# The two ends of a causal attention stage: no stacks to fill, matmuls over 48 and 51 rows, the second sequence prepared between the first one's maxima, the last two sequences written out

## The reference, cut to what matters

```python
qkv = jnp.einsum('bsi,oi->bso', layernorm(x), W_qkv)      # B = 16, S = 512, 128 channels
Q, K, V = heads(qkv)                                      # 16 heads of 8 channels
Q, K = apply_rope(Q), apply_rope(K)
scores = jnp.einsum('bhqd,bhkd->bhqk', Q, K) / sqrt(8)
scores = where(causal, scores, -inf)
out = softmax(scores, -1) @ V
x = x + out.reshape(B, S, 128) @ W_o.T
```

## Time and profile before

| | |
|---|---|
| median of three executions | 2770.93 us |
| the profiled execution's own time | 2778.27 us |
| its span | 2776.3 us |
| busy: PE, DVE, ACT, POOL | 82%, 71%, 52%, 45% |
| attention, first DVE instruction | 120.98 us |
| attention, first matmul of the loop | 208.85 us |
| attention, last DVE instruction starts | 1072.74 us |
| next stage, first DVE instruction | 1081.88 us |

### The profile page before, as it was taken

The page is one execution under the profiler, slowest core; times in us unless marked ns, Lnnn a source line. Parts: engine busy times, 40 slices in busy tenths (PEclk is TensorE's granted clock), DMA queues, the critical chain, the costliest instruction groups (busy, mean ns, idle before and its releaser), DMA issues. The chain is left out here.

```text
span 2776.3 us, 50795 instructions
## 1 busy us (share of the span) xinstructions
PE 2284.9 (82%) x14828; PEld 1682.9 (61%) x14828; DVE 1964.2 (71%) x5225; ACT 1446.4 (52%) x2918; POOL 1258.7 (45%) x1094
## 2 busy tenths in 40 slices
PE   6559998999899896768898989488987889898990
PEld 5425555555555554756776777367776667677770
DVE  6766676676676665778786766368887877776775
ACT  4205454454554554756665656355553767565660
POOL 3242322231231222527773555457775387645551
PEclk8759999999999998888899999789999888999995
DMA  2022122122212213411125656310100011356656
GB/s 66 15 36 35 25 36 36 26 31 34 33 25 36 37 25 81 159 54 35 43 73 181 215 205 214 103 31 23 30 15 22 22 39 42 127 187 213 213 198 182
DMA packets 140590, 222.36 MB, mean 80 GB/s; under 512 B 21326, under 2 KB 100992, under 8 KB 129883
## 3 DMA queue, kind: packets, MB, share of 16 engines
q1 hardware_dynamic: 122203, 185.46, 24.7%
q0 software_dynamic: 18176, 34.14, 3.6%
HBM read 136.75 MB, written 57.32 MB: 70 GB/s over the span
## 5 line engine op out<-in xcount | busy, mean ns | idle before, releaser
L955 DVE TENSOR_REDUCE attn_rowmax<-psum 128x1 f32<-128x512 f32 (+3 forms) x748 | 457.5, 637 | 262.0 <-PE psum L796 259.2
L740 ACT ACTIVATE attn_probs<-psum 128x512 f32<-128x512 f32 (+1 forms) x704 | 385.2, 560 | 463.8 <-PE psum L859 453.6
L794 PE MATMUL psum<-attn_ks,attn_qs 72*128 72x512 bf16 (+3 forms) x1088 | 314.0, 324 | 32.5 <-DVE attn_rowmax L955 25.9
L857 PE MATMUL psum<-attn_qs,attn_ks 75*128 75x512 bf16 (+3 forms) x1024 | 290.5, 316 | 32.1 <-issue 19.7
L1290 POOL DMA_INDIRECT experts_answers<-ffn1a_y_rows,ffn1a_out_row x156 | 156.1, 1001 | 150.9 <-ACT ffn1a_y_rows L1360 110.8
L796 PE MATMUL psum<-attn_mask_qk,attn_ident_b 128*128 128x128 bf16 x1088 | 224.0, 231 | 0.0
L1290 POOL DMA_INDIRECT experts_answers<-ffn1b_y_rows,ffn1b_out_row x156 | 154.3, 989 | 147.7 <-ACT ffn1b_y_rows L1360 109.9
L655 POOL TENSOR_TENSOR attn_rstd<-attn_var_eps,minus_half 128x4 f32<-128x4 f32 x18 | 18.3, 1018 | 423.7 <-DVE attn_var_eps L932 423.7
L859 PE MATMUL psum<-attn_mask_kq,attn_ident_b 128*128 128x128 bf16 x1024 | 206.3, 226 | 0.0
L794 PEld LDWEIGHTS psum<-attn_ks,attn_qs 72*128 72x128 bf16 x1088 | 112.6, 103 | 135.2 <-DVE attn_rowmax L955 82.4
L1658 DVE TENSOR_TENSOR ffn1a_hl<-ffn1a_h,ffn1a_hh 128x1024 fp32r<-128x1024 f32 x142 | 174.0, 1225 | 11.3 <-issue 0.9
(11 more groups left out here) (425 smaller groups left out, 6447.7 us busy)
## 6 DMA issues: line engine op xcount, KB each, us to landing
ffn1a_w_ring<-experts_packed SPq DMA_DIRECT2D x39, 1026.5 KB, 5.1
ffn1b_w_ring<-experts_packed SPq DMA_DIRECT2D x39, 1026.5 KB, 5.1
attn_qs<-attn_qparts SPq DMA_DIRECT2D x216, 64.0 KB
attn_ks<-attn_kparts SPq DMA_DIRECT2D x216, 64.0 KB
ffn1a_x_in<-experts_slots SPq DMA_DIRECT2D x39, 264.0 KB, 4.8
ffn1b_x_in<-experts_slots SPq DMA_DIRECT2D x39, 264.0 KB, 4.8
gla_answers<-experts_answers SPq DMA_DIRECT2D x32, 256.0 KB, 3.1
ffn1b_h<-experts_answers SPq DMA_DIRECT2D x16, 512.0 KB, 5.5
```

The lines of the kernel that those rows point to most:

```text
L740: act.activation(probs[:, slot_of(j), 0:n], ps_exp[j % 2][:, 0:n], ACT.Exp, scale=SCALE).then_inc(exp_ready, 1)
L794: pe.matmul(out, qs[k][0:K_QK, 4 * g + hh, qt * P:(qt + 1) * P], ks[k][0:K_QK, 4 * g + hh, 0:n_keys], start=True, stop=False)
L857: pe.matmul(out, ks[k][:, 4 * g + hh, kt * P:(kt + 1) * P], qs[k][:, 4 * g + hh, kt * P:N], start=True, stop=False)
L955: dve.tensor_reduce(rowmax[:, NT - 1 - w, h:h + len(heads)], score_bank(n, j)[:, 0:len(heads) * width_of(w)].rearrange("p (a c) -> p a c", ...
```

## The change

1. `K_QK` becomes 48 and `K_ALL` 51. The maxima's parts stand in rows 48 to 50. No stack is filled any more: a new array `minus_one` (3 x 16 x 512, bf16) is sent to rows 48 to 50 of both `ks` by two more DMAs at the start. `set_values` keeps the memsets of `v_aug`. In the built program each matmul carries the part of the array that it uses: for `score` and `exponent` that was 128 x 128 and is 64 x 128 now; the mask matmuls between them stay at 128 x 128.
2. POOL splits the first sequence's queries and keys in one go. The second sequence's `turn`, `project`, `values`, `normalise_x` and `rotate` move in between the first one's 44 units.
3. The body becomes a function `sequence(i, k, following, prepare)`. The loop has seven bodies, and sequences 14 and 15 are written out: 14 prepares nothing, 15 neither prepares nor scores. `is_first` asks for n == 0, since numbers are now given for the last ones too.

```diff
-    K_QK = 72
+    K_QK = len(PAIRS) * DH
@@ SP
+            for k in range(2):
+                sp.dma_start(ks[k][K_QK:K_ALL, :, :], w["minus_one"]).then_inc(weights_in, 16)
...
-            sp.wait_ge(stacks_set[0], 4)
             stack(0, 0, 1)
             stack(1, 0, 1)
-            sp.wait_ge(stacks_set[1], 4)
             stack(0, 1, 2)
             maxima(0, 0, 0)
             stack(1, 1, 2)
-            with sp.Fori(0, BODIES) as i:
+            with sp.Fori(0, BODIES - 1) as i:
...
+            maxima(1, 0, NB - 2)
+            maxima(0, 1, NB - 1)
+            maxima(1, 1, NB - 1)
             for f in range(2):
-                sp.wait_ge(stack_in[f], 16 * BLOCKS * (NB + 2))
+                sp.wait_ge(stack_in[f], 16 * BLOCKS * NB)
@@ POOL
             inverse_std(1)
-            set_stacks(pool, 0, ((ks, -1.0),), True)
-            split(1, None, (0,))
+            set_values(pool, 0)
+            split(1, None)
             inverse_std(2)
-            split(1, None, (1,))
-            set_stacks(pool, 1, ((ks, -1.0),), True)
+            set_values(pool, 1)
             split(2, 1)
@@ PE, ahead of the loop
-            for k in range(2):
-                turn(k + 1)
...
+            turn(1)
+            pe.wait_ge(weights_in, N_WEIGHTS)
+            project(0, 1)
+            project(1, 1)
+            values(1)
             for j in range(UNITS):
                 score(0, 0, j)
+                if j == E_TURN:
+                    pe.wait_ge(v_read, 1)
+                    turn(2)
+                if j == E_Q:
+                    project(0, 2)
+                if j == E_K:
+                    project(1, 2)
+                if j == E_V:
+                    values(2)
@@ PE, DVE and ACT, in a sequence
                     for j in range(UNITS):
                         exponent(j)
-                        score(1 - k, s + 1, j)
+                    if following:
+                        score(1 - k, s + 1, j)
...
-                        if j == E_TURN:
+                    if j == E_TURN and prepare:
                             turn(s + 3)
...
+            with pe.Fori(0, BODIES - 1) as i:
+                for k in range(2):
+                    sequence(i, k, True, True)
+            sequence(BODIES - 1, 0, True, False)
+            sequence(BODIES - 1, 1, False, False)
```

More of the change, by code:

```diff
@@ L554, in attention_stage @@
         weights_in = sem("weights_in")
-        stacks_set = [sem(f"stacks_set{k}") for k in range(2)]
+        values_set = [sem(f"values_set{k}") for k in range(2)]
         var_ready = sem("var_ready")
@@ L636, in _, with set_values @@
                             maxima(0, 1 - k, i * 2 + (k + 1))
+            maxima(1, 0, NB - 2)
+            maxima(0, 1, NB - 1)
+            maxima(1, 1, NB - 1)
             for f in range(2):
-                sp.wait_ge(stack_in[f], 16 * BLOCKS * (NB + 2))
[L639 to L649, removed]
+                sp.wait_ge(stack_in[f], 16 * BLOCKS * NB)
+                sp.wait_ge(m_in[f], 16 * NB)
+        def set_values(engine, k):
+            engine.memset(v_aug[k][:, :, :, :], 0.0).then_inc(values_set[k], 1)
+            engine.drain()
+            engine.memset(v_aug[k][:, :, :, DH:DH + 1], 1.0).then_inc(values_set[k], 1)
         @block.gpsimd
@@ new lines, in sequence, with read_o @@
+            def sequence(i, k, following, prepare):
+                s = i * 2 + k
+                def read_o(g):
+                    act.wait_ge(pv_done, s * GROUPS + (g + 3))
+                    act.wait_ge(oT_psum, s * 4 + (g + 2))
+                    act.activation(oT[:, :], ps_o[g % 2], ACT.Copy).then_inc(o_read, 1)
+                for j in range(UNITS):
+                    g, (kt, heads) = j // RING, FILLS[j % RING]
+                    n = len(heads) * width_of(kt)
+                    act.wait_ge(exp_psum, s * UNITS + (j + 1))
+                    if j % RING == 0:
+                        act.wait_ge(pv_done, s * GROUPS + (g + 1))
+                    act.activation(probs[:, slot_of(j), 0:n], ps_exp[j % 2][:, 0:n], ACT.Exp,
+                                   scale=SCALE).then_inc(exp_ready, 1)
+                    if j == 0:
+                        end_of(s)
+                    if j == 2 and following:
+                        values(1 - k)
+                    if j == A_TOKENS:
+                        tokens_of(s)
+                    if j == A_TURN and prepare:
+                        turn(s + 3)
+                    if j == A_V and prepare:
+                        read_v(s + 3)
+                    if j in A_O:
+                        read_o(A_O.index(j))
@@ L843, in _ @@
             pe.wait_ge(mT_ready, 1)
-            with pe.Fori(0, BODIES) as i:
-                for k in range(2):
[L846 to L892, removed]
-                        score(1 - k, s + 1, j)
[L894 to L903, removed]
-                        if j == E_TURN:
-                            turn(s + 3)
-                        if j == E_Q:
-                            project(0, s + 3)
-                        if j == E_K:
-                            project(1, s + 3)
-                        if j == E_V:
-                            values(s + 3)
-                        if j == E_HALF:
-                            pe.wait_ge(v_read, s + 3)
-                            turn_maxima(0, s + 1)
-                        if j in E_O:
-                            turn_o(E_O.index(j))
-                    weigh(GROUPS - 1)
@@ L1002, in _ @@
             dve.drain()
-            for s in range(2):
-                moments(s * NT)
-                normalise_x(s * NT, s + 1)
-                if s == 0:
-                    set_stacks(dve, 0, ((qs, 0.0),), False)
-                    dve.wait_ge(weights_in, N_WEIGHTS)
-                rotate(0, s + 1)
-                rotate(1, s + 1)
-            set_stacks(dve, 1, ((qs, 0.0),), False)
+            moments(0)
+            normalise_x(0, 1)
+            dve.wait_ge(weights_in, N_WEIGHTS)
+            rotate(0, 1)
+            rotate(1, 1)
+            moments(NT)
             for j in range(UNITS):
                 row_max(0, j)
+                if j == V_NORM:
+                    normalise_x(NT, 2)
+                if j in (V_Q, V_Q + 1):
+                    rotate(0, 2, (j - V_Q,))
+                if j in (V_K, V_K + 1):
+                    rotate(1, 2, (j - V_K,))
                 if j == UNITS // 2 - 1:
@@ new lines, in sequence @@
+            def sequence(i, k, following, prepare):
+                s = i * 2 + k
+                for j in range(UNITS):
+                    if following:
+                        row_max(s + 1, j)
+                    if j == 1 and prepare:
+                        moments((s + 2) * NT)
+                    if j == V_MAXIMA:
+                        read_maxima(1, s)
+                    if j == V_LAST_O:
+                        normalise(o_heads, channels_of(3), s * 4 + 2)
+                    if j == V_NORM and prepare:
+                        normalise_x((s + 2) * NT, s + 3)
+                    if j == V_OUT:
+                        add_out(s)
+                    if j in (V_Q, V_Q + 1) and prepare:
+                        rotate(0, s + 3, (j - V_Q,))
+                    if j in (V_K, V_K + 1) and prepare:
+                        rotate(1, s + 3, (j - V_K,))
+                    if j in V_O:
+                        g = V_O.index(j)
+                        normalise(o_heads, channels_of(g), s * 4 + (g + 3))
+                    if j == V_HALF and following:
+                        split_maxima(0)
+                    if j == V_HALF_READ and following:
+                        read_maxima(0, s + 1)
+                if following:
+                    split_maxima(1)
@@ L1046, in _ @@
+            with dve.Fori(0, BODIES - 1) as i:
+                for k in range(2):
+                    sequence(i, k, True, True)
+            sequence(BODIES - 1, 0, True, False)
+            sequence(BODIES - 1, 1, False, False)
             normalise(o_heads, channels_of(3), NB * 4 + 2)
@@ L2207, in layout @@
     c["mask_qk"] = np.triu(np.full((P, P), BIG, np.float32), 1).astype(bf)
+    c["minus_one"] = np.full((3, 16, SEQ), -1.0, np.float32).astype(bf)
     c["mask_kq"] = np.tril(np.full((P, P), BIG, np.float32), -1).astype(bf)
```

148 lines of the change are left out of this document (79 added, 69 removed).

## The result

The changed kernel takes 3402.26 us (median of 4, 3391.31 to 3414.93), 1.228 times the kernel before (interval 1.2249 to 1.2314), against a forecast of 3053 us in a range up to 3200. In that comparison the kernel before took 2769.51 us: 633 us more, where I had forecast 282. Direction and place were right, the size was less than half of what came.

What follows compares the result with a forecast made beforehand. PE was taken to bound the loop. Start +9.5, tile changes +293, sequence 14 -4, sequence 15 -11 and handover -5.5 gave +282 on the median 2770.9: 3053 us, range 2738 to 3200 (8 in 10).

Steps and rivals of the forecast that it cites:

- the price of a change: PE's score and exponent matmuls against masks: each change of tile size costs 0.09 us, 256 a sequence, 23.0 us.
- +19.5 for sequences 0 to 14: Loop sequences: 23.0 us of tile changes less 3.5 in PE's waits, +19.5 each, +293 us over 15.
- rival C: A change dearer than between column tiles (3337 us at 0.16), or the clock falls (3250 at three tenths); chance 0.14.
- Part 2, the start: First sequence: first score at 162.3, exponent 2 us earlier, then tile changes of +11.5; together +9.5 us.
- my 39.3: First maxima, with the second sequence's preparation between them: 29.3 us plus 10, from 162.3 to 201.6.
- my 4.5 to 6.6: Start: the DMA of the maxima's parts goes at about 202 and lands 4.5 to 6.6 us later.
- my 11.5: Start: 128 changes of tile size at 0.09 us each, +11.5 us.
- Part 3, the end: Sequence 14 without preparation -4 us, sequence 15 without scores -11 with tile changes, handover to the next stage -5.5.
- -9.5 for -4: Sequence 14: dropping its preparation was to save 4 us, after what lay in waits.
- My 34 for it: Sequence 15 without tile changes: ACT bounds it at 34 us where 53.1 was taken before, so -19.
- Rival B: Changes between row tiles are free, so only the two ends count: -30.5 us, 2740 in all; chance 0.18.
- my 42: Sequence 15 with tile changes: PE bounds it at 42 us, so -11.

Runs made afterwards that it cites:

- ends_75: The changed kernel with 72 and 75 rows again, filled by four DMAs at the start, both ends still changed: 2732.9 us, 0.990 of the kernel before.
- rows_48: The kernel before with only the rows changed, to 48 and 51, old ends kept: 3451.3 us, 1.250 of the kernel before.
- mask_64: The changed kernel with each mask matmul cut into two over 64 rows: 2952.4 us, 1.069 of the kernel before.
- ends_128: The changed kernel with both ends kept and rows filled up to 125 and 128 with zeros against minus ones: 2720.6 us, 2716.1 when run again.
- tail_75: The kernel before with only the last two sequences written out, old start and 72 and 75 rows kept: 2736.1 us, 0.990 of the kernel before.

## Why the prediction was wrong

**Part 1, the direction and the price of a change: right.** I took 0.09 us from column tiles; it is 0.10, by the starts, at the upper clock level and 0.11 at the lower (a pair of L797 and L799 takes 0.76 us from 160.76 to 161.52 in the changed kernel; the same pair takes 0.53 in ends_75: 160.30 to 160.83). The drain that the Trainium skill states in TensorEngine Tiling (Array Packing), Key Properties, holds for rows as well: the trace agrees, with the overlap at 0.07 us in place of 0.16. Nearly all of today's waits were used up: L797's waits for the maxima are gone. The changes are 252 more a sequence, from 8 to 260: so far 252 x 0.105 - 3.5 = 23.0 us a sequence instead of 19.5.

**Part 1, "+19.5 for sequences 0 to 14": the step that failed.** Between ends_75 and the changed kernel the start of sequence 14 moves from 943.3 - 203.8 = 739.5 us to 1540.4 - 214.8 = 1325.6 behind that of sequence 0: 41.9 us a sequence. 23.0 are the changes. The other 18.9, some 280 us over 15 sequences, are what is left, and the clock is the term that the sum put at nothing: 0.653 for 0.961. I had the clock in rival C, with a price of 65 us for each tenth of the time at 0.50, a chance of 0.14 for the whole rival and three tenths as its example, and left it out of the forecast because no row tied it to the change. With its two levels at 1.00 and 0.50, a mean of 0.653 is 0.69 of the time at 0.50, and 0.961 is 0.08: six tenths more, 400 us by that price. So the price was high enough, and the share was what I had not seen coming. rows_48 shows the loss of time and of clock with the rows alone, mask_64 that the clock falls with few changes too, ends_128 that it goes with the rows in use. What it follows in the changed kernel, the gaps at the changes or the smaller part of the array, no run separates. Rows 6 held a warning: PE ran without a gap at 0.50 over 72 rows, so a PE without gaps was not enough to bring the clock up.

**Part 2, the start.** `xn` 2.4 us for 3, the first score at 160.8 for 162.3, the DMA of the maxima at once: right. Without the changes of tile I had -2; it is -4 (ends_75 against tail_75). The maxima with the preparation between them take 39.6 us in ends_75 (159.81 to 199.40) for my 39.3; most of the other two us are in the DMA of the maxima, issued at 199.83 and landed by 202.98, in 3.2 us for my 4.5 to 6.6. That the length came right is partly luck: PE was not fully busy there before, as I had it (5.4 us of the 8 from 182 to 190), and in ends_75 the clock rises for a while (0.91 from 170 to 174), where in tail_75 it stays at 0.50 up to the first `exponent`. The changes cost 10.3 us there for my 11.5: from the first `xn` to the first `exponent` it is 89.6 us in the changed kernel (124.25 to 213.89) and 79.3 in ends_75.

**Part 3, the end.** By the first exponentials of the sequences, from the kernel before to ends_75, 14 goes from 52.9 to 43.4 us: -9.5 for -4. In the kernel before its clock was 0.90 (965.0 to 1017.9), in ends_75 1.00 (943.3 to 986.7); a tenth below 1.00 is a fifth of the 52.9 us at 0.50, which costs half of that, 5.3 us by estimate, and leaves 4.2 for the preparation. Sequence 15 goes from 47.7 to 36.3 us: -11.4 for -19. My 34 for it is near; the 53.1 that I took it from was a window from 1015 to 1068.1, longer than the sequence at both ends. In ends_75 neither engine bounds it alone: of the 36.3 us PE is busy for 28.8 and ACT for 24.8, PE waits for ACT for 5.9 and ACT for PE for 13.6. The sum, -21, is near my -23 because two misses cancel: luck. The handover is 3.05 us, as said. So Rival B's -30.5 for the ends, against the 28 of ends_75, is right as a sum and not in its terms. In the changed kernel itself sequence 15 takes 52.8 us for my 42, at 0.68 of the clock: the same missing term.

**The range.** It reached 3200 because I gave C 0.14. The changed kernel is C by its size, and by the second of its two mechanisms, the clock; the first one, that the overlap is lost whole, did not come.

## What to carry to other kernels

A matmul over 64 rows or fewer in a stream of others over 128 pays about 0.1 us at each border, both ways: keep the contraction above 64 rows, with zeros if need be. To narrow the whole stream (mask_64) took back 450 of 669 us and was still 7% slower than the kernel before. When an edit makes PE's work thinner, ask for the clock too; where the trace shows PE without gaps at the lower level, that is a warning. Here zeros up to 128 rows make a kernel that beats both: 2716 us, 1.9% less than the kernel before beside it. And compare such stretches by their distance from the start of the work, in more than one execution.

## What the hardware showed that I had not expected

The granted clock went with the rows in use, though the added rows were zeros: in the body 0.940 and 0.961 with 72 and 75 rows, 0.975 and 0.983 with 125 and 128, and over the whole kernel 0.909 to 0.915 against 0.922 to 0.928 in six executions each. With nearly all matmuls on 64-row tiles (mask_64) it was 0.835 with PE about as dense as before. Whether the rows or the size of the tile does it there is open; no run holds one of them still. A change of tile size costs 0.09 us of overlap between row tiles as between column tiles, and at such a change the next weights are loaded only 4 ns ahead of their matmul; whether that is the cause or goes with it, no run here tells.
